# Macaron block: the last batch's row scatters and the second group's zero rows spread over the last run of blocks, the first group's zero rows moved behind a layer norm's factors

## The chip, the cores and the metric

One core of a Trainium2 chip. The metric is device time in microseconds, the median of the runs shown.

## The reference

Eight sequences of 256 tokens, 128 channels. Three sublayers, each on a layer norm (no learned scale) of the residual x:

```python
x = x + 0.5 * ffn(layernorm(x))
x = x + attention(layernorm(x))
x = x + 0.5 * ffn(layernorm(x))      # same weights as the first
```

The attention has 16 heads of 8 channels, rotary embedding, an ALiBi bias (0 for later keys, so it is not causal) and a projection with a bias. The feed-forward is a mixture of 8 experts, 128 to 352 and back, top 2 by a softmax over the router's 8 logits:

```python
scores = softmax(xt @ router_w); w, idx = top_k(scores, 2)
h = gelu(xt @ w1[e]) * (xt @ v1[e]);  y = h @ w2[e]
out = sum over the two chosen e of w * y + bias
```

## The kernel before, in words

The 2048 tokens are 16 tiles of 128 rows. Of the first feed-forward, four tiles are computed densely (all experts), which is the dense stage at the start. The other twelve, and all sixteen of the second feed-forward, are routed: each normalised row is written twice, with a number behind its 128 floats (516 bytes), into a buffer `xs[p]` in HBM, at a place (`pos`) that sorts rows by expert. The blocks of 128 rows of one expert are then loaded from there, sent through the expert, and the result rows are scattered to `yp[p]` by their numbers (`dest`). The last block of an expert is filled up with rows of zeros. There are three such phases p: 0 is the first feed-forward (31 blocks), 1 is batches 0 to 5 of the second (31 blocks), 2 is its batches 6 and 7 (15 blocks).

The order of the work is written out by hand, engine by engine. PE: dense stage; blocks 0 to 30; attention over batches b = 0 to 7, each in 16 slots s; then the last run of 46 blocks, 31 to 76, in steps i = 0 to 45 (`blocks(1)`). During batch b, the layer norm and routing of the batch before for the second feed-forward are fitted in. The rest of batch 7 (projection, layer norm, routing) lies inside the first steps of the last run (`last_attention`).

A block passes through: load by SP (L418, six slots, three blocks a group); three transposes on PE for a group (L1462); an exact split into high and low parts, ACT (L756) and DVE (L1131 next to it copies `dest`); up projections on PE (L1472 to L1474); gelu on ACT (L783), product on DVE (L1156); transposes of the hidden rows on PE (L1483), copies out on DVE (L1137) and ACT (L763); down projection on PE (L1490); copy of y on ACT (L770); scatter of y on POOL (L538).

`y_copy` of block n waits until the scatter of block n - 3 has landed (three slots `ysb`), and the transposes L1483 of a block wait for the copy of y of the block two before it (two banks). SP's first load of a phase waits in `rows_there` until all of the phase's row scatters and zero rows have landed and its table is made.

POOL issues all indirect DMAs, in its one order:

- `scatter(r, c, ...)` (L523, DMA at L531): one DMA for each copy k of each tile, so four for a batch of two tiles. `scatter2(b)` is called for it in the second feed-forward.
- `zero_scatter(p)` (L569): two DMAs, 128 single rows (L573) and 128 groups of 8 rows, 4,128 bytes each (L576), 528 KB in all.
- `y_scatter(n)` (L535, DMA at L538): 128 rows of 512 bytes.

In the pass of POOL's loop for batch 7 it issues: `scatter2(5)`, `zero_scatter(1)`, two iotas (`number_pairs(6)`), the layer norm's factors of batch 6 (`rstd_of`, four small operations L516 to L521), an iota, `copy_again(6)`. After the loop comes `scatter2(6)`, and then the last run: `y_scatter` of each block, with batch 7's four row scatters behind those of steps 8 and 9, two each, `zero_scatter(2)` behind that of step 10, and four additions to the residual (`add_ffn_bias`, L593) behind steps 12 to 15. What those feed: SP's load of block 62 (the first of phase 2, used by PE in step 30), and DVE's `combine`, which begins in step 38.

Of the kernel before, what the change touches and what calls it, by code (L numbers as in the profile page):

```python
# [14 lines left out]
B, N, D = 8, 256, 128  # L15
P = 128
TB = N // P
NT = B * TB
# [28 lines left out]
ZG = 8  # L47
# [74 lines left out]
def macaron(nc, x, small_w, w1, v1, w2, ffn_bias, proj_b, slopes, ident, dist, dist_t, rope, expert_ids,  # L122
            far, ones_rows, out):
    ctx = ExitStack()
    with ctx:
        ctx.enter_context(nc.allow_low_precision(reason="exact splits"))

        def sb(name, shape, dt=F32):
            return ctx.enter_context(nc.sbuf_tensor(name, shape, dt))

        def sem(name):
            return ctx.enter_context(nc.semaphore(name))

        def sems(name, n):
            return [ctx.enter_context(nc.semaphore(f"{name}{i}")) for i in range(n)]
# [104 lines left out]
        zpos = sb("zpos", [P, 2, 1], U32)  # L240
# [18 lines left out]
        xs = [nc.dram_tensor(f"xs{r}", (BLOCK_ROWS * P + P, XW), F32, kind="Internal").ap() for r in range(3)]  # L259
# [42 lines left out]
        zstep, zero_landed, zmem = sems("zstep", 2), sems("zero_landed", 2), sem("zmem")  # L302
# [3 lines left out]
        scat1, scat2 = sem("scat1"), sems("scat2", 2)  # L306
# [39 lines left out]
        def xn2_twice(b, k):  # L346

            return ((xn2_again_l if b >= SPLIT else xn2_again) if k else xn2)[:, b % 2]
# [162 lines left out]
        def _(pool):  # L511
            def rstd_of(w, c, first_tile, tiles):

                t = slice(first_tile, first_tile + tiles)
                pool.wait_ge(mean_done[w], (c + 1) * tiles)
                nc.gpsimd.tensor_scalar(rstd[:, t], mv[:, t, 1], EPS, None, ALU.add).then_inc(eps_done[w], 1)  # L516
                nc.gpsimd.tensor_scalar(nmr[:, t], mv[:, t, 0], -1.0, None, ALU.mult).then_inc(eps_done[w], 1)
                pool.wait_ge(eps_done[w], 2 * c + 2)
                nc.gpsimd.tensor_tensor(rstd[:, t], rstd[:, t], mhalf[:, 0:tiles], ALU.pow).then_inc(rstd_done[w], 1)
                pool.wait_ge(rstd_done[w], c + 1)  # L520
                nc.gpsimd.tensor_tensor(nmr[:, t], nmr[:, t], rstd[:, t], ALU.mult).then_inc(nmr_done[w], 1)  # L521

            def scatter(r, c, src, landed, tiles=None):  # L523

                T = CHUNKS[r][0]
                p = 2 if r and c >= SPLIT else r
                pool.wait_ge(pos_done[r], c + r)
                pool.wait_ge(again_done[r], c + r)
                for t in tiles or range(c * T, (c + 1) * T):
                    for k in range(2):  # L530
                        nc.gpsimd.indirect_dma_start(  # L531
                            out=xs[p][:, :], out_offset=bass.IndirectOffsetOnAxis(ap=pos[:, k, t:t + 1], axis=0),
                            in_=src(t, k), in_offset=None).then_inc(landed, 16)
# [8 lines left out]
            def number_pairs(b):  # L542

                if b >= 2:
                    pool.wait_ge(scat2[b % 2], 64 * (b // 2))
                for k in range(2):
                    nc.gpsimd.iota(xn2_twice(b, k)[:, :, D].bitcast(U32), [[P, TB]], base=b * 2 * N + k * N, channel_multiplier=1
                                   ).then_inc(numbers_at, 1)
# [6 lines left out]
            def split_qk(b, step):  # L555

                r, rs_ = (rc_e, rsn_e) if b < 2 else (rc, rsn)
                if step == 0:
                    pool.wait_ge(cos_done, b + 1)
                    pool.wait_ge(sin_done, b * 2 + 2)  # L560
                    nc.gpsimd.tensor_tensor(r, r, rs_, ALU.add).then_inc(split_step, 1)
                elif step == 1:
                    pool.wait_ge(split_step, b * 5 + 2)
                    nc.gpsimd.tensor_tensor(r, r, lev[:, 0], ALU.subtract).then_inc(split_step, 1)
                else:
                    pool.wait_ge(split_step, b * 5 + 4)
                    nc.gpsimd.tensor_tensor(lev[:, 2], r, lev[:, 1], ALU.subtract).then_inc(split_step, 1)

            def zero_scatter(p):  # L569
                r, zeros = min(p, 1), zero_rows2 if p else zero_rows1  # L570
                pool.wait_ge(zstep[r], 18 if p == 2 else 9)
                pool.wait_ge(numbered, 4 if p else 3)
                nc.gpsimd.indirect_dma_start(  # L573
                    out=xs[p][:, :], out_offset=bass.IndirectOffsetOnAxis(ap=zpos[:, 0, :], axis=0),
                    in_=zeros[:, ZG, :], in_offset=None).then_inc(zero_landed[r], 16)
                nc.gpsimd.indirect_dma_start(  # L576
                    out=xs[p].rearrange("(g z) d -> g (z d)", z=ZG),
                    out_offset=bass.IndirectOffsetOnAxis(ap=zpos[:, 1, :], axis=0),
                    in_=zeros[:, 0:ZG, :].rearrange("p z w -> p (z w)"), in_offset=None).then_inc(zero_landed[r], 16)

            def project_bias(b):

                pool.wait_ge(xn_done[1], 2 * b + 2)
                nc.gpsimd.tensor_tensor(xres[:, 2 * b:2 * b + 2, :], xres[:, 2 * b:2 * b + 2, :],
                                        pbias[:, None, :].broadcast_to([P, TB, D]), ALU.add).then_inc(pb_added, 1)

            def add_ffn_bias(r, q):
                if q == 0:
                    if r == 0:
                        nc.gpsimd.tensor_scalar(hbias[:, :], hbias[:, :], 0.5, None, ALU.mult).then_inc(half_done, 1)  # L590
                        pool.wait_ge(half_done, 1)
                pool.wait_ge(xn_done[2 * r], 4 * q + 4)
                nc.gpsimd.tensor_tensor(xres[:, 4 * q:4 * q + 4, :], xres[:, 4 * q:4 * q + 4, :],  # L593
                                        hbias[:, None, :].broadcast_to([P, 4, D]), ALU.add).then_inc(bias_added, 1)
# [43 lines left out]
            for c in range(1, 4):  # L638
                scatter(0, c, lambda t, k: xn1[:, t - DT, k, :], scat1)
            zero_scatter(0)  # L640
            for q in range(1, 4):
                add_ffn_bias(0, q)
# [31 lines left out]
                    split_qk(1, 2)  # L674

            rstd_of(1, 2, 4, TB)
            def scatter2(b, tiles=None):
                scatter(1, b, lambda t, k: xn2_twice(t // TB, k)[:, t % TB, :], scat2[b % 2], tiles)

            for b in range(B):  # L680
                if b + 2 < B:
                    project_bias(b + 2)
                if b >= 2:
                    scatter2(b - 2)
                if b == B - 1:
                    zero_scatter(1)
                if b == 0:
                    rstd_of(1, 3, 6, TB)
                if b + 2 < B:
                    for step in range(3):  # L690
                        split_qk(b + 2, step)
                if b >= 1:
                    number_pairs(b - 1)
                    rstd_of(2, b - 1, 2 * b - 2, TB)
                if b >= 1 and b + 3 < B:
                    rstd_of(1, b + 3, 2 * b + 6, TB)
                if b == B - 2:

                    pool.wait_ge(s2_full, 16 * (B - 2))
                    nc.gpsimd.memset(zero_rows2, 0.0).then_inc(zmem, 1)  # L700
                    pool.wait_ge(zmem, 7)
                    nc.gpsimd.iota(zero_rows2[:, :, D].bitcast(U32), [[1, ZG + 1]], base=SCRAP, channel_multiplier=ZR
                                   ).then_inc(numbered, 1)
                if b == B - 1:

                    pool.wait_ge(s2_full, 16 * (B - 1))
                    nc.gpsimd.iota(run[2][:, 0, :], [[REG, E]], base=0, channel_multiplier=0,
                                   allow_small_or_imprecise_dtypes=True).then_inc(numbered, 1)
                if b >= 1:
                    copy_again(b - 1)  # L710
            scatter2(B - 2)
            for n in range(FIRST[1], sum(NB)):
                y_scatter(n)
                i = n - FIRST[1]
                if i == 0:
                    number_pairs(B - 1)
                    rstd_of(2, B - 1, 2 * B - 2, TB)
                if i == 3:
                    copy_again(B - 1)
                if 8 <= i < 10:  # L720
                    scatter2(B - 1, [NT - 2 + i - 8])
                if i == 10:
                    zero_scatter(2)
                if 12 <= i < 16:
                    add_ffn_bias(1, i - 12)


        @block.scalar
# [1036 lines left out]
```

## Time and profile before

| | us |
|---|---|
| median of 3 runs | 482.81 |
| lowest, highest | 482.15, 485.86 |
| span of the profiled execution, first to last instruction | 502.7 |

No separate time of the profiled execution is given beside its span. The profile has for each engine its instructions in order of time, the idle time before each in brackets with what released it. "issue" there is idle time in which the engine waited for nothing that the profile shows, and "remote", like "another core or an unknown queue", a release whose source has no record. The granted clock of TensorE is 1.00 at 2.4 GHz and 0.50 at 1.2 GHz. Some records can be missing.

### The profile page before, as it was taken

The numbers are of one execution on the slowest core, as the hardware profiler recorded it, in microseconds if no ns is written. First come the engines' busy times: TensorE is split into PE (matmuls) and PEld (weight loads), VectorE is DVE, ScalarE is ACT, GpSimd is POOL, SyncE is SP. The second block draws the span as 40 slices with busy tenths as digits, with TensorE's granted clock in tenths as the row PEclk, the third lists the DMA queues.
The fourth block names the chain that finished last, engine by engine and source line by source line (L and its number), as shares of the span: only waits on it lengthen the run. The fifth ranks groups of instructions, "written<-read, shape, count | busy, mean of one in ns | idle before, by whom it ended". The sixth has DMA issues, their size and how long they took to land.

```text
span 502.7 us, 10906 instructions
## 1 busy us (share of the span) xinstructions
PE 441.0 (88%) x3447; PEld 369.0 (73%) x3447; DVE 311.2 (62%) x935; ACT 248.2 (49%) x585; POOL 237.4 (47%) x321
## 2 busy tenths in 40 slices
PE   1998859899999898699999999999779969999990
PEld 1877648788899775577777777777459958888880
DVE  3765645976867485295959586756526744544672
ACT  4744434436444456255556565555465524554541
POOL 7365658556453413044454545432525467534441
PEclk9999959999999999899999999999999989999997
DMA  8971111122331010230212120200112223122522
GB/s 236 290 116 38 48 58 33 50 75 75 91 85 54 30 48 15 71 85 17 60 50 61 47 63 30 64 24 3 70 37 61 64 60 96 53 65 72 171 80 78
DMA packets 50633, 35.51 MB, mean 71 GB/s; under 512 B 5754, under 2 KB 47706, under 8 KB 50538
## 3 DMA queue, kind: packets, MB, share of 16 engines
q1 hardware_dynamic: 45140, 23.90, 18.9%
q0 software_dynamic: 4784, 10.54, 6.3%
q8 instruction: 30, 0.49, 0.4%
q10 hardware_dynamic: 656, 0.40, 0.3%
q14 instruction: 23, 0.19, 0.1%
HBM read 15.37 MB, written 13.01 MB: 56 GB/s over the span
## 4 chain that ended last, share of the span: by engine, by line
PE 65%; DVE 9%; issue 8%; ACT 5%; POOL 4%; DMA 3%; another core or an unknown queue 2%; ACTq 1%; SPq 1%; POOLq 0%; DVEq 0%
PE bank L1490 9%; PE bank L1483 6%; PE bank L1587 5%; PE bank L1472 5%; PE bank L1473 4%; PE bank L1474 4%; PE bank L1626 4%; PE bank L1611 4%; PE bank L1444 3%; PE bank L1590 2%; PE bank L1591 2%; PE bank L1462 2%; PE bank L1614 2%; PE bank L1434 2%
## 5 line engine op out<-in xcount | busy, mean ns | idle before, releaser
L538 POOL DMA_INDIRECT yp<-scr,dest x77 | 76.5, 994 | 90.8 <-ACT scr L770 71.1
L877 ACT ACTIVATE stage<-bank 128x512 f32<-128x512 f32 x128 | 74.6, 597 | 72.6 <-PE bank L1615 63.7
L1263 DVE TENSOR_REDUCE nm<-bank 128x2 f32<-128x512 f32 x128 | 84.0, 685 | 38.4 <-PE bank L1591 35.8
L1490 PE MATMUL bank<-wd,scr 128*128 (+1 forms) x462 | 64.9, 277 | 1.3 <-ACT scr L763 1.3
L1472 PE MATMUL bank<-wu,xbT 128*128 x154 | 63.1, 410 | 2.1 <-DVE xbT L1129 1.8
L1137 DVE COPY scr<-bank 128x256 f32<-128x256 f32 x77 | 32.5, 422 | 51.5 <-PE bank L1483 22.8
L1490 PEld LDWEIGHTS bank<-wd,scr 128*128 128x128 f32 (+1 forms) x462 | 60.7, 193 | 1.8 <-issue 1.7
L1587 PE MATMUL bank<-qk_rows 126*128 126x256 bf16 x256 | 50.8, 280 | 4.9 <-DMA qk_rows<-lev 4.2
L1611 PE MATMUL bank<-qk_rows 128*128 128x256 bf16 x256 | 50.3, 279 | 3.7 <-DMA qk_rows<-wd 3.0
L1473 PE MATMUL bank<-wu,xbT 128*128 x154 | 50.8, 330 | 0.0
L1474 PE MATMUL bank<-wu,xbT 128*128 x154 | 50.8, 330 | 0.0
L783 ACT ACTIVATE scr<-bank 128x352 f32<-128x352 f32 x77 | 35.7, 463 | 29.1 <-PE bank L1474 21.7
L1483 PE MATMUL bank<-idn,scr 128*128 128x128 f32 (+1 forms) x231 | 40.1, 283 | 10.0 <-ACT scr L770 8.7
L1614 PE MATMUL bank<-near_hi,idn_r 128*128 128x256 f32 x128 | 47.3, 369 | 0.0
L1590 PE MATMUL bank<-near_hi,idn_r 128*128 128x256 f32 x128 | 47.0, 367 | 0.0
L1156 DVE TENSOR_TENSOR scr<-bank,scr 128x352 f32<-128x352 f32 x77 | 40.1, 521 | 9.4 <-ACT scr L783 2.1
L763 ACT ACTIVATE scr<-bank 96x128 f32<-96x128 f32 x77 | 21.0, 273 | 47.9 <-DVE scr L1137 33.9
L1483 PEld LDWEIGHTS bank<-idn,scr 128*128 128x128 f32 (+1 forms) x231 | 25.1, 138 | 23.0 <-issue 14.7
L1615 PE MATMUL bank<-near_lo,idn_r 128*128 128x256 f32 x128 | 36.0, 281 | 0.0
L1591 PE MATMUL bank<-near_lo,idn_r 128*128 128x256 f32 x128 | 35.8, 280 | 0.0
L531 POOL DMA_INDIRECT xs<-qk_rows,pos x28 | 27.4, 980 | 15.9 <-issue 9.9
L1626 PE MATMUL bank<-stage,vaug 128*9 128x256 f32 x512 | 34.2, 385 | 0.4 <-ACT stage L877 0.4
(218 smaller groups left out, 949.3 us busy)
## 6 DMA issues: line engine op xcount, KB each, us to landing
qk_rows<-lev SPq DMA_DIRECT2D x96, 64.0 KB
scr<-xs SPq DMA_DIRECT2D x77, 64.5 KB
stage<-yp SPq DMA_DIRECT2D x8, 256.0 KB, 3.2
scr<-yp SPq DMA_DIRECT2D x6, 256.0 KB, 3.1
stage<-in_w SPq DMA_DIRECT2D x8, 176.0 KB, 3.4
stage<-in_v SPq DMA_DIRECT2D x8, 176.0 KB, 4.3
xs<-qk_rows SPq DMA_DIRECT2D x3, 451.5 KB
yp<-scr,dest POOLq DMA_INDIRECT x77
```

The lines of the kernel that those rows point to most:

```text
L538: nc.gpsimd.indirect_dma_start(out=yp[PHASE[n]][:, :], out_offset=bass.IndirectOffsetOnAxis(ap=dest[:, n:n + 1], axis=0), in_=ysb[:, n % Y ...
L877: nc.scalar.activation(probs[:, g % RING, kt, 2 * (hp % 2):2 * (hp % 2) + 2, :], psS2[(b * 16 + j) % 3][:, :].rearrange("p (h n) -> p h n" ...
L1263: nc.vector.tensor_reduce(nm[:, qt, 2 * hp:2 * hp + 2], psS1[i % 2][:, :].rearrange("p (h n) -> p h n", h=2), AX.X, ALU.max, negate=True). ...
L1472: nc.tensor.matmul(dst, hi, moving(n, a), start=True, stop=False)
L1473: nc.tensor.matmul(dst, lo, moving(n, a), start=False, stop=False)
L1474: nc.tensor.matmul(dst, hi, moving(n, a + 2 * F), start=False, stop=True).then_inc(done, 1)
L1483: i = nc.tensor.transpose(ph[n % len(ph)][0:w, k * P:(k + 1) * P], hid[:, n % 2, f:f + w], idn[:, :])
L1490: i = nc.tensor.matmul(ph[n % len(ph)][:, 3 * P:4 * P], hTs[0:w, n % 2, k * P:(k + 1) * P], wd[0:w, bass.ds(experts[n], 1), k, :].rearrang ...
L1587: nc.tensor.matmul(o[:, j * N:(j + 1) * N], qs[b % RING][0:S1_ROWS, h, qt * P:(qt + 1) * P], ks[b % RING][0:S1_ROWS, h, :], start=(j == 0) ...
L1590: nc.tensor.matmul(o, idn_r[:, :], near_hi[0][:, 2 * hp:2 * hp + 2, :], start=False, stop=False)
L1611: nc.tensor.matmul(o[:, a * N:(a + 1) * N], ks[b % RING][0:S2_ROWS, h, kt * P:(kt + 1) * P], qs[b % RING][0:S2_ROWS, h, :], start=(a == 0) ...
L1614: nc.tensor.matmul(o, idn_r[:, :], near_hi[1][:, 2 * hp:2 * hp + 2, :], start=False, stop=False)
```

## The change

- Batch 7's four row scatters, before behind `y_scatter` of steps 8, 8, 9, 9, are issued one each behind steps 8, 10, 12 and 14. `scatter` and `scatter2` get a parameter `copies` for it.
- The two DMAs of `zero_scatter(2)`, before both behind step 10, are issued behind steps 17 and 20 (`half`).
- The four additions `add_ffn_bias(1, q)` move from steps 12 to 15 to steps 21 to 24.
- `zero_scatter(1)` moves from before `number_pairs(6)` and `rstd_of(2, 6, ...)` to behind them.

No DMA or instruction is added or removed.

```diff
-            def scatter(r, c, src, landed, tiles=None):
+            def scatter(r, c, src, landed, tiles=None, copies=range(2)):
...
-                    for k in range(2):
+                    for k in copies:
...
-            def zero_scatter(p):
+            def zero_scatter(p, half=None):
...
+                if half != 1:
+                    nc.gpsimd.indirect_dma_start(... zpos[:, 0, :] ...)
+                if half != 0:
+                    nc.gpsimd.indirect_dma_start(... zpos[:, 1, :] ...)
...
                 if b >= 2:
                     scatter2(b - 2)
-                if b == B - 1:
-                    zero_scatter(1)
                 if b == 0:
                     rstd_of(1, 3, 6, TB)
...
                 if b >= 1:
                     number_pairs(b - 1)
                     rstd_of(2, b - 1, 2 * b - 2, TB)
+                if b == B - 1:
+                    zero_scatter(1)
...
-                if 8 <= i < 10:
-                    scatter2(B - 1, [NT - 2 + i - 8])
-                if i == 10:
-                    zero_scatter(2)
-                if 12 <= i < 16:
-                    add_ffn_bias(1, i - 12)
+                if i in (8, 10, 12, 14):
+                    scatter2(B - 1, [NT - 2 + (i - 8) // 4], [(i - 8) // 2 % 2])
+                if i in (17, 20):
+                    zero_scatter(2, (i - 17) // 3)
+                if 21 <= i < 25:
+                    add_ffn_bias(1, i - 21)
```

## Rows read from the trace of the kernel before

**Rows 1.** The page: span, busy shares, and the chain that ended last.

```profile
span 502.7 us, 10906 instructions
...
PE 441.0 (88%) x3447; PEld 369.0 (73%) x3447; DVE 311.2 (62%) x935; ACT 248.2 (49%) x585; POOL 237.4 (47%) x321
...
PE 65%; DVE 9%; issue 8%; ACT 5%; POOL 4%; DMA 3%; another core or an unknown queue 2%; ACTq 1%; SPq 1%; POOLq 0%; DVEq 0%
```

**Rows 2.** Busy time by stretch: four bursts of DMAs on POOL.

```profile
core 0: us, PE busy (x) PEld busy (x) DVE busy (x) ACT busy (x) POOL busy (x), PEclk, DMA share, GB/s
...
54.87:67.20 12.33, 7.83 (x49) 6.33 (x47) 6.42 (x24) 3.59 (x10) 9.57 (x10) 0.92 0.15 49
234.50:239.40 4.90, 4.90 (x42) 4.39 (x39) 2.78 (x6) 2.23 (x5) 3.97 (x4) 1.00 0.12 40
354.31:362.40 8.09, 4.81 (x47) 3.48 (x46) 4.17 (x18) 4.17 (x9) 6.55 (x7) 0.99 0.14 44
402.20:411.30 9.10, 4.28 (x31) 3.76 (x31) 3.60 (x14) 2.20 (x7) 5.75 (x6) 0.93 0.24 68
```

**Rows 3.** POOL in order of time, in the last run of blocks.

```profile
402.22 0.96 POOL L538 DMA_INDIRECT yp<-scr,dest  x1 [1.56 <-ACT scr L770]
...
406.01 0.96 POOL L538 DMA_INDIRECT yp<-scr,dest  x1 [0.30 <-issue]
...
408.53 0.96 POOL L531 DMA_INDIRECT xs<-qk_rows,pos  x1 [0.30 <-issue]
411.36 0.96 POOL L538 DMA_INDIRECT yp<-scr,dest  x1 [1.86 <-ACT scr L770]
...
419.40 1.29 POOL L593 TENSOR_TENSOR xres<-xres,hbias 128x512 f32<-128x512 f32 x1
```

**Rows 4.** PE in order of time in the same stretch: the transposes of hid.

```profile
411.23 0.87 PE L1483 MATMUL bank<-idn,scr 128*128 128x128 f32 x3 [4.39 <-ACT scr L770]
...
415.58 0.84 PE L1483 MATMUL bank<-idn,scr 128*128 128x128 f32 x3
...
418.29 0.52 PE L1483 MATMUL bank<-idn,scr 128*128 128x128 f32 x3
...
420.43 0.52 PE L1483 MATMUL bank<-idn,scr 128*128 128x128 f32 x3
```

**Rows 5.** ACT there: the copy of y that PE waited for.

```profile
410.80 0.28 ACT L770 ACTIVATE scr<-bank 128x128 f32<-128x128 f32 x1 [2.15 <-remote]
```

**Rows 6.** Busy time of each engine in two stretches at half clock.

```profile
362.20:365.70 3.50, 3.28 (x24) 2.10 (x24) 1.12 (x5) 1.25 (x3) 0.99 (x6) 0.51 0.37 151
410.00:416.90 6.90, 5.67 (x24) 5.54 (x25) 2.44 (x8) 2.13 (x6) 3.83 (x4) 0.51 0.30 107
```

**Rows 7.** POOL in order of time, last attention batch.

```profile
361.38 0.96 POOL L576 DMA_INDIRECT xs<-qk_rows,zpos  x1 [0.30 <-issue]
...
366.35 0.20 POOL L521 TENSOR_TENSOR nmr<-nmr,rstd 128x2 f32<-128x2 f32 x1
```

**Rows 8.** PE in order of time, last attention batch to the last run.

```profile
362.42 1.22 PE L1650 MATMUL bank<-wsm,scr 128*128 128x128 f32 x4 [2.55 <-issue]
...
373.93 0.52 PE L1462 MATMUL bank<-idn,scr 128*128 128x128 f32 x3 [0.35 <-issue]
```

**Rows 9.** ACT in the dense stage: gelus 1, 23 and 24.

```profile
15.69 0.60 ACT L842 ACTIVATE scr<-bank 128x512 f32<-128x512 f32 x1
...
84.21 0.60 ACT L842 ACTIVATE scr<-bank 128x512 f32<-128x512 f32 x1 [1.10 <-PE bank L1436]
...
86.50 0.59 ACT L842 ACTIVATE scr<-bank 96x512 f32<-96x512 f32 x1 [1.11 <-PE bank L1436]
```

**Rows 10.** What DMA moved, in 40 slices of 0.3 us from 361 us on.

```profile
GB/s 0 0 220 0 0 0 303 385 399 427 248 0 0 0 0 0 0 0 41 157 59 141 78 136 50 46 172 29 131 96 181 5 0 0 0 0 0 0 0 0
```

**Rows 11.** SP issuing loads, up to 367 us: the first three.

```profile
365.59 1.53 SPq L418 DMA_DIRECT2D scr<-xs  x3
```

**Rows 12.** The chain that ended last: the last y scatter's data.

```profile
492.22 2.33 DMA yp<-scr,dest
```

More of the change, by code:

```diff
@@ L572, in zero_scatter @@
                 pool.wait_ge(numbered, 4 if p else 3)
[L573 to L579, printed above, removed]
+                if half != 1:
+                    nc.gpsimd.indirect_dma_start(
+                        out=xs[p][:, :], out_offset=bass.IndirectOffsetOnAxis(ap=zpos[:, 0, :], axis=0),
+                        in_=zeros[:, ZG, :], in_offset=None).then_inc(zero_landed[r], 16)
+                if half != 0:
+                    nc.gpsimd.indirect_dma_start(
+                        out=xs[p].rearrange("(g z) d -> g (z d)", z=ZG),
+                        out_offset=bass.IndirectOffsetOnAxis(ap=zpos[:, 1, :], axis=0),
+                        in_=zeros[:, 0:ZG, :].rearrange("p z w -> p (z w)"), in_offset=None).then_inc(zero_landed[r], 16)
             def project_bias(b):
@@ L676, in _, with scatter2 @@
             rstd_of(1, 2, 4, TB)
-            def scatter2(b, tiles=None):
-                scatter(1, b, lambda t, k: xn2_twice(t // TB, k)[:, t % TB, :], scat2[b % 2], tiles)
+            def scatter2(b, tiles=None, copies=range(2)):
+                scatter(1, b, lambda t, k: xn2_twice(t // TB, k)[:, t % TB, :], scat2[b % 2], tiles, copies)
             for b in range(B):
```

## Prediction

> **What bounds the kernel now.** I read the page first: PE is busy 88% of a span of 502.7 us and holds 65% of the chain that ended last, but "issue" and an unknown source together hold 10% of that chain [rows 1]. So the question is where PE stands still for reasons no engine explains. I then went through POOL in order of time, looked for its bursts of DMAs, and asked for the busy time of each engine in those stretches [rows 2]. The reader is to see this: in a burst of four DMAs (234.50 to 239.40, the ordinary batch; there are five like it before 340 us) PE is busy 4.90 us of 4.90. In the burst that four row scatters make with the first group's two zero DMAs, PE is busy 4.81 of 8.09; in the burst of the last run 4.28 of 9.10; in the dense stage's longest, of ten, 7.83 of 12.33. Short bursts cost nothing, long ones stop PE in their later half.
>
> The last run's burst in detail: POOL's six DMAs from 402.22 to 409.49 follow one another with 0.30 us between [rows 3]; PE stands for 4.39 us before the transposes at 411.23 [rows 4], released by ACT's copy of y at 410.80, which itself stood 2.15 us for a "remote" release [rows 5]. That copy has two waits, the down projection on PE and the landing of a scatter of y issued eleven microseconds earlier, both over by then; its source has no record. After it the clock is granted at 0.51 for the stretch 410.0 to 416.9 [rows 6]. The other: PE stands 2.55 us until 362.42, put down to "issue" [rows 8], and the clock is 0.51 from 362.2 to 365.7 [rows 6].
>
> **Are these stalls in the timed runs too?** The profiled execution took 502.7 us, the median of the runs is 482.81: 19.9 us of the span (or more, since what lies around the span is only in the timed run) are not there without the recorder. PE's steady stretches run at the full clock and nothing can be taken from them. The dense stage goes from gelu 1 at 15.69 to gelu 24 at 86.50, 70.8 us; at the undisturbed 2.29 us of its last step [rows 9] 23 steps take 52.7. So 18.1 us are over there, most of it around bursts. With the two stalls above (11.0 us, below) that makes 29.1 us of stalls, against 19.9 us that the timed runs don't have. If all of the excess is stalls, (29.1 - 19.9) / 29.1 = 0.32 of a traced stall is real; some of the dense stage's 18.1 us are ordinary waits for loads and routing, which lowers that. I take 0.25. The ends are 0 (the recorder alone makes them) and 1.
>
> A rule of the Trainium skill bears on this (NOTIFIC — the notification-queue block, section 7.1): the block that writes trace records holds back its sources rather than lose a record inside, and that can throttle an engine. The "remote" releases without a record [rows 5] fit it and don't prove it; by that rule alone the share is 0 and the sum below comes to 483.9. Another page speaks against it (Runtime: NRT & Kernel Launch, on the preamble and postamble): a profile's total is about 6.2 us above the reported time for reasons of its own. If this span contained that, only 13.7 us of the excess were stalls, the share were 0.53 and the sum near 478; no row here shows it.
>
> **Part 1, the last run.** Nothing is removed: six DMAs and four additions are moved.
> - The stall. PE lost 4.39 us [rows 4]. Behind it, two blocks at half clock: 411.23 to 415.58 is 4.35 us, where such a step, with the transposes of a group, takes some 0.4 more than 2.14, say 2.5, and 415.58 to 418.29 is 2.71 against 2.14 from 418.29 to 420.43 [rows 4]: 1.8 + 0.6 = 2.4. Together 6.8 us in the trace.
> - The new order. A block takes 2.14 us or, every third, 2.5; a DMA on POOL 0.96 + 0.30 = 1.26 [rows 3]. With one more behind every second block POOL is busy 3.8 of some 4.5 us and has at most three in a row, fewer than the four that cost nothing [rows 2]. So the stall goes whole.
> - A true wait that goes, recorder or not. Without the stall, the scatters would follow at 1.26 us: step 9's at 406.01, step 10's at 409.8, the zeros at 411.1 and 412.3, step 11's at 413.6. The zeros' data take 2.9 us (below), so step 11's rows, in the same queue behind them, land near 416.2. The copy of y in step 14's turn, six blocks after that of step 8 (402.0 at latest, since its scatter began at 402.22 [rows 3]), is due at 402.0 + 6 x 2.27 = 415.6. So about 0.6 us of real waiting, passed on to PE. Bounds: 0 (a scatter passes the zeros' data) and 1.8 (each addition of 1.29 us [rows 3] pushes the next scatter as well; those four fall 3 to 4.3 us behind their copies, against a slack of 6.8 - 0.3 - 2.3 = 4.2 us, the 2.33 being a scatter's data [rows 12]). Afterwards, the additions lie behind steps 21 to 24 and start from no backlog: at most some 2 us late, hidden by the same slack.
> - The zeros in steps 17 and 20 must have landed before SP loads block 62, which PE wants in step 30; at 2.9 us of data behind step 20 they have over seven steps, 15 us. Batch 7's rows land by step 16. Both hidden. The additions are wanted in step 38. Hidden too. If I am wrong on the queue, the cost is a load that waits, not PE.
>
> **Part 2, the first group's zeros.** They leave a burst of six, which becomes a burst of four like those that cost nothing [rows 2]. In the trace this gives 2.55 us [rows 8] and half of the 3.28 busy us at half clock [rows 6], 1.6: 4.2 together. Lower bound 0, if PE then waits for the same chain through ACT.
>
> What it costs. Before, the large zero DMA is issued at 361.38 [rows 7] and its data move until 364.3: the slices at 303 to 427 GB/s, the seventh to the eleventh of 0.3 us from 361 [rows 10]. SP waits for that. It issues three loads from 365.59 on [rows 11]; the 193.5 KB of the three have moved seven slices after the traffic begins at 366.4, at 368.5 [rows 10]. PE wants them at 373.93 [rows 8]: 5.4 us in hand. After, the pair starts when the factors are done, 366.35 + 0.20 = 366.55 [rows 7]: large DMA at 366.55 + 0.30 + 0.96 + 0.30 = 368.1, data gone at + 2.9 = 371.0, three loads there at + 4.2 = 375.2. PE's own work behind the factors doesn't shrink (366.55 to 373.93 is 7.4 us, nearly all at full clock), and if the stall before is gone both move forward together. So PE waits 375.2 - 373.9 = 1.3 us at the head of the last run, and nothing covers it: all 46 blocks stand behind that load. With a quarter chance that the idle brings one more stretch at half clock like [rows 6], 0.4. I take 1.7; bounds 0 (SP answers the last landing at once, which saves the 1.3 us from 364.3 to 365.59) and 3.3 (1.3 + 1.6 + 0.4 of semaphores). Also queued behind the two DMAs on POOL are an iota and `copy_again(6)`, half a microsecond later than now, before row scatters that begin at 375: hidden.
>
> **Sum.** In the trace: 502.7 - 6.8 - 4.2 + 1.7 = 493.4. For the median: a quarter of 11.0 is 2.75; 482.81 - 2.75 - 0.6 + 1.7 = 481.2 us.
>
> **Rivals.**
> 1. The stalls are real in timed runs (share 1). For it: engines stop in every long burst in the same way, and the clock falls, which is no artefact of records. Against it: the 19.9 us, and the missing source. 482.81 - 11.0 + 1.7 = 473.5.
> 2. The late zeros take over (slower). Place: SP's wait at the head of the last run. Stalls all the recorder's, the queue's wait 0, the full 3.3 us: 486.1. If the landing comes 1.7 us later still, because the zeros' data now meet the attention's last work, it passes the 1% bound: near 488. It decides from the point where zeros land more than 3.1 us after the factors (373.93 less 4.2 us of loads, less 366.55). For it: the 5.4 us in hand and the 6.7 us by which the DMA moves are both in rows. Against: the loads may be issued quicker.
> 3. The change does nothing that counts: the stalls are the recorder's, and the true wait and the late zeros cancel: 482.8.
>
> **How the numbers follow.** Forecast (share near a quarter, 479 to 484.5) 0.50; rival 1 and shares above one half 0.23; rival 2 0.14, half of it above the 1% bound; rival 3 0.13. A change under 1% is what a measurement of this kernel can hardly tell from none. Faster by over 1% (under 478.0): rival 1, 0.23, and a little of the forecast's lower end, 0.02: 0.25. Slower by over 1% (above 487.6): 0.07. Within: 0.68. The range leaves out the far ends of rivals 1 and 2: 474.5 to 486.
>
> **What would show it.** In the changed kernel's profile, POOL should have no run of more than four DMAs behind 350 us; PE's gaps of 4.39 and 2.55 us and their stretches at 0.51 should be gone; SP's first load of the last run should start near 372 by today's clock (5 to 6 us behind the factors) and the transposes L1462 behind it should wait over 1 us for a DMA. The forecast is wrong if the span shrinks by 9 us and the time as well (rival 1), if the time rises although the stalls went (rival 2), or if a new PE gap shows at steps 20 to 25.

## The result and the profile after

The changed kernel takes 488.04 us (median of 12 runs, 485.73 to 490.21) against 483.82 us for the kernel before (12 runs, 482.15 to 486.98). The ratio on record is 1.0077, 95% interval 1.0051 to 1.0103: 0.8% slower, some 3.7 us. (The two medians are 4.2 us apart; this text goes by the ratio.) The forecast was 481.2 us, no change or slightly faster, range 474.5 to 486.0; the time lies outside it, near what rival 2 gave (486.1 to 488). The kernel before itself measured 1.0 us above the 482.81 us of three runs that the sum began with.

The profiled execution of the changed kernel, the page's first line and its chain by engine (for [rows 1]):

```profile
span 486.1 us, 10909 instructions
...
PE 56%; DVE 7%; DMA 6%; issue 5%; ACT 5%; POOL 3%; SPq 2%; ACTq 1%; POOLq 0%; DVEq 0%
```

Its span is 486.1 us beside a timed 488.01 of the same execution: 1.9 us lie around the span. By that, as an estimate, the execution profiled before, 502.7 us [rows 1], would have had a time of 504.6, while none of the 12 timed runs is above 486.98. The "remote" share of the chain is gone. DMA has 6% of it where it had 3%, and the wait at the head of the last run is in it. The chain from the factors of the layer norm to the last run's first transposes (columns: start, us, what; "..." stands for lines left out):

```profile
353.99 0.20 POOL nmr L521
354.18 0.53 issue
354.71 1.08 POOL xs L574
355.79 0.30 issue
356.10 3.33 DMA xs<-qk_rows,zpos
...
359.56 0.47 SPq L351
...
360.30 0.35 SPq L418
...
361.50 1.85 DMA scr<-xs
363.35 0.27 issue
363.62 0.89 PE bank L1464 x3
```

PE has nothing else to do while this chain runs out, from 360.22 on: factors done at 354.19, small zero DMA, large zero DMA, 3.33 us until its data have landed, SP reads the table and issues three loads, the third takes 1.85 us to land, PE transposes. In the kernel before the large zero DMA was issued ahead of the factors, and all of this lay under the attention's last slots.

PE in order of time, the same transposes (for [rows 8], where they waited 0.35 us):

```profile
363.62 0.87 PE L1464 MATMUL bank<-idn,scr 128*128 128x128 f32 x3 [3.40 <-DMA scr<-xs]
...
369.28 0.49 PE L1485 MATMUL bank<-idn,scr 128*128 128x128 f32 x3
```

And the busy time by stretch behind the wait (for [rows 6]; PE first, PEclk the third figure from the end):

```profile
363.60:369.10 5.50, 4.22 (x15) 3.78 (x16) 1.46 (x5) 2.24 (x3) 2.32 (x3) 0.50 0.49 111
369.10:380.00 10.90, 10.90 (x83) 10.22 (x83) 7.64 (x24) 6.38 (x19) 4.61 (x9) 1.00 0.16 41
```

The granted clock is 0.50 from 362.3, while PE still waits, until 369.1, so the first blocks run at half clock. In the last run POOL now has at most three DMAs in a row (for [rows 3]), and PE's transposes there follow at 2.13 and 2.5 us without a gap (the next wait is 0.57 us for a load, at 455.36):

```profile
405.77 0.95 POOL L538 DMA_INDIRECT yp<-scr,dest  x1 [1.17 <-ACT scr L772]
407.03 0.96 POOL L531 DMA_INDIRECT xs<-qk_rows,pos  x1 [0.30 <-issue]
408.29 0.95 POOL L538 DMA_INDIRECT yp<-scr,dest  x1 [0.30 <-issue]
410.03 0.96 POOL L538 DMA_INDIRECT yp<-scr,dest  x1 [0.79 <-ACT scr L772]
```

### The profile page after: what moved, and what is told of

Same layout as the page of the kernel before. It is cut to its first block, busy times and chain, and to the rows that moved or that the text cites. A ratio compares the mean times of both kernels' runs of the same rounds, so it can differ in the third digit from the quotient of the medians.

```text
span 486.1 us, 10909 instructions
## 1 busy us (share of the span) xinstructions
PE 435.6 (90%) x3447; PEld 365.4 (75%) x3447; DVE 313.7 (65%) x935; ACT 248.1 (51%) x585; POOL 236.7 (49%) x321
## 4 chain that ended last, share of the span: by engine, by line
PE 56%; DVE 7%; DMA 6%; issue 5%; ACT 5%; POOL 3%; SPq 2%; ACTq 1%; POOLq 0%; DVEq 0%
PE bank L1492 8%; PE bank L1485 6%; PE bank L1589 5%; PE bank L1474 4%; PE bank L1475 4%; PE bank L1476 4%; PE bank L1613 4%; PE bank L1628 4%; PE bank L1592 3%; PE bank L1593 2%; PE bank L1464 2%; PE bank L1616 2%; PE bank L1617 2%; DMA scr<-xs 2%; DMA qk_rows<-wd 2%
## 5 line engine op out<-in xcount | busy, mean ns | idle before, releaser
L1628 PE MATMUL bank<-stage,vaug 128*9 128x256 f32 x512 | 35.2, 395 | 0.4 <-ACT stage L879 0.4
L772 ACT ACTIVATE scr<-bank 128x128 f32<-128x128 f32 x77 | 21.3, 276 | 23.9 <-PE bank L1492 23.9
```

## The experiments

Two theories at the start. Late zeros: the loss is the first group's zero rows, whose landing nothing covers any more. Spreading: the DMAs put between the blocks cost. Ratios are to the kernel before, timed beside each version on the same chip, with the 95% interval. Where two versions are compared with each other by their ratios, both intervals count.

### The kernel before, profiled again

No edit.

> The kernel before itself, for a second profile and for what no change measures as. If the two long stalls (PE 4.39 us at 406 to 411, 2.55 us at 360 to 362) and the dense stage's 18 us belong to one profiled execution alone, this profile's span lies near 482 us and PE has no gap over 1 us in either place. If they come with every profile, the span is again near 500 and the gaps are there. Ratio to the kernel before 1.000, within 0.002.

Measured: 483.94 us against 484.02, ratio 1.0007 (0.9981 to 1.0034). The second profile, first line of the page, and PE and ACT in the last run:

```profile
span 479.9 us, 10906 instructions
```

```profile
396.55 0.52 PE L1483 MATMUL bank<-idn,scr 128*128 128x128 f32 x3
399.92 0.52 PE L1483 MATMUL bank<-idn,scr 128*128 128x128 f32 x3 [0.83 <-ACT scr L770]
402.06 0.52 PE L1483 MATMUL bank<-idn,scr 128*128 128x128 f32 x3
```

```profile
399.50 0.28 ACT L770 ACTIVATE scr<-bank 128x128 f32<-128x128 f32 x1 [1.03 <-DMA yp<-scr,dest]
```

The same kernel, 22.8 us shorter in its span: the stalls of 4.39 and 2.55 us [rows 4, 8] are not in this execution, and POOL here issues eleven DMAs with 0.30 us between, 385.57 to 399.17, in the same place. So long bursts do not stop PE. What the burst does here is the small true wait of the prediction: step 14's copy of y waits 1.03 us for a scatter to land (step 11's, issued at 396.95), and PE 0.83 us for the copy.

The dense stage, too, was stretched in the first profile alone. Gelus 1 and 24 in the second (for [rows 9], where they stand at 15.69 and 86.50):

```profile
15.68 0.60 ACT L842 ACTIVATE scr<-bank 128x512 f32<-128x512 f32 x1
...
73.91 0.59 ACT L842 ACTIVATE scr<-bank 96x512 f32<-96x512 f32 x1 [1.11 <-PE bank L1436]
```

It takes 58.2 us and not 70.8: 12.6 us of the 22.8 lie here. In all profiles but the first it is 57.6 to 58.9 us, the changed kernel's too. So of the 18.1 us above the ideal 52.7, some 5.5 are in every profile.

### One part at a time

Only the last run's part (`e1`), which takes back in the changed kernel:

```diff
                     scatter2(b - 2)
+                if b == B - 1:
+                    zero_scatter(1)
...
                     rstd_of(2, b - 1, 2 * b - 2, TB)
-                if b == B - 1:
-                    zero_scatter(1)
```

> Only the last run's part of the change: the first group's zeros back ahead of the layer norm's factors. Theory (late zeros): the whole loss lies in them, so this is as fast as the kernel before or up to 0.6 us faster, ratio 0.998 to 1.001, and PE has no wait for a load at the head of the last run. Rival (spreading): the DMAs between the blocks cost, ratio 1.005 or more.

Only the first group's zeros (`e2`), the opposite edit on the kernel before:

> Only the first group's zeros moved, the last run as before. Late zeros: ratio 1.008 (3.7 us: a wait of 3 us or more for the first load, and one more stretch at half clock). Spreading: ratio 1.000 to 1.002.

Measured: e1 483.32 us, ratio 0.9982 (0.9960 to 1.0004); e2 488.08 us, ratio 1.0087 (1.0069 to 1.0106). The last run's first transposes in e1, then in e2:

```profile
359.91 0.52 PE L1464 MATMUL bank<-idn,scr 128*128 128x128 f32 x3 [0.35 <-issue]
```

```profile
361.80 0.52 PE L1462 MATMUL bank<-idn,scr 128*128 128x128 f32 x3 [3.45 <-DMA scr<-xs]
```

In e2 PE waits 3.45 us for the first loads, and the clock is 0.50 for 6.8 us there; in e1 the transposes wait 0.35 us as before. The loss is the second part's, whole. Spreading costs nothing: its ratio is what PE's 0.83 us would give, though the interval just reaches 1.

### The landing moved earlier and later

`e4`, the changed kernel with the large DMA of the pair ahead of the factors and the small one behind:

```diff
+                if b == B - 1:
+                    zero_scatter(1, 1)
...
-                    zero_scatter(1)
+                    zero_scatter(1, 0)
```

> The changed kernel with the large zero DMA back ahead of the factors and only the small one (128 rows) behind them. Late zeros: the small one starts at the changed kernel's 354.7 and lands about 2.3 us later instead of at 359.4, so SP loads 2.4 us earlier; the wait for the first load falls from 3.4 to about 1 us and the loss to a third, ratio 1.002 to 1.004. If only the order against the factors counts and not the landing, the ratio stays at 1.008.

`e5`, the kernel before with the pair one step later than the change has it:

```diff
                 if b >= 1:
                     copy_again(b - 1)
+                if b == B - 1:
+                    zero_scatter(1)
```

> The kernel before with the first group's zeros one step later than the change puts them: behind copy_again(6), which waits for the normalised rows. Late zeros with nothing to cover them: PE's wait for the first load grows by what the large zero DMA starts later (about 0.9 us by the changed kernel's rows), so 4.3 us against 3.4, and the time by as much, ratio 1.010 to 1.011. If the loss came from the clock alone or from the factors' place, it stays at 1.0087.

Measured: e4 484.37 us, ratio 0.9995 (0.9965 to 1.0026), e5 490.04 us, ratio 1.0104 (1.0067 to 1.0142). The first transposes of the last run in e4 and in e5:

```profile
359.88 0.52 PE L1466 MATMUL bank<-idn,scr 128*128 128x128 f32 x3 [1.23 <-DMA scr<-xs]
```

```profile
364.19 0.88 PE L1462 MATMUL bank<-idn,scr 128*128 128x128 f32 x3 [4.72 <-DMA scr<-xs]
```

The landing of the pair's last DMA sets the wait, not the factors' place. The last DMA starts 1.91 us behind the end of the factors in the changed kernel and 3.21 us behind it in e5 (353.43 to 356.64): 1.30 us more, and the wait grows by 1.32. Nothing absorbs any of it. (In time e5 is 1.0104 beside e2's 1.0087; that difference is inside the noise.) In e4 the last DMA starts 0.52 us behind the factors (352.62 to 353.14), and being the small one it is also done sooner: 6.74 us from its start to PE's transposes and not 7.52. Of the 2.17 us less wait, 1.39 are the earlier start and 0.78 the smaller DMA. e4's time is better than I expected (1.002 to 1.004, of which its interval holds the lower part): its wait, 0.88 us above the 0.35 of e1, is about what the spreading gives back.

### The clock behind the wait

PE is kept at work where it waits by matmuls whose result nothing reads, into a bank that is free there. `e6` is the changed kernel with 28 of them before the first transposes and 10 behind; `e7` is e1 with 2 and 10; `e10` the kernel before with 2 and 10.

```diff
+            def keep_busy(n):
+                for _ in range(n):
+                    nc.tensor.matmul(bank[0][:, 0:N], ks[1][0:S2_ROWS, 0, 0:P], qs[1][0:S2_ROWS, 0, :], start=True, stop=True)
...
             ranks(1, B - 2, rank2)
+            keep_busy(28)
             blocks(1)
...
                 xbT(GROUP_OF[first])
+                if r == 1:
+                    keep_busy(10)
```

> The changed kernel with PE kept at work while it waits at the head of the last run: 28 matmuls of 256 columns into a bank that is free then, before the first transposes, and 10 behind them (in the 1.26 us in which it waits for DVE); none of them is used. They make the wait no shorter. If the fall to half clock (0.50 from 362.3 to 369.1) is a part of the loss, the clock stays at 1.00 there and the time falls by 1.5 to 2.5 us against the changed kernel, ratio to before 1.003 to 1.005. If the clock costs nothing, the ratio stays at 1.008.

> Only the last run's part of the change (as in e1), with PE kept at work at the head of the last run by 2 unused matmuls before the first transposes and 10 behind them. The clock was 0.50 for 3.4 us there in e1's profile and 1.00 in the second profile of the kernel before; if it falls in most executions, this is worth some 1.4 us (the first transposes of a hidden row 4.1 us behind PE's arrival and not 5.5) on top of e1's 0.9: ratio 0.995 to 0.997. If it falls seldom, ratio 0.998 as e1.

> The kernel before with nothing but the 2 and 10 unused matmuls at the head of the last run. e7 was at 0.9951 with both parts, e1 at 0.9982 with the spreading alone. If the two add, this is at 0.997 (1.4 us, when the fall to half clock behind 361 us comes in nearly all executions); if it comes in few, 0.999 or more.

Measured: e6 485.71 us, ratio 1.0020 (0.9993 to 1.0046). PE, and the busy time behind the wait, in e6's profile:

```profile
363.59 0.52 PE L1468 MATMUL bank<-idn,scr 128*128 128x128 f32 x3 [0.99 <-DMA scr<-xs]
...
367.36 0.49 PE L1489 MATMUL bank<-idn,scr 128*128 128x128 f32 x3
```

```profile
363.60:369.10 5.50, 5.33 (x40) 4.81 (x41) 2.63 (x8) 3.36 (x6) 1.92 (x2) 1.00 0.41 97
```

The loads come no sooner: counted from the end of the factors (353.48), the transposes start 10.11 us later and not 9.43, because the third load took 2.56 us in this execution and not 1.85. The 0.99 us are what the 28 matmuls left of the wait. The clock stays at 1.00, and the first transposes of hidden rows come 3.77 us behind those of the input and not 5.66 (363.62 to 369.28 above). So 1.89 us of the loss are the half clock. The time agrees, less sharply: the medians are 2.3 us apart, the ratios 0.0057, which is 2.8 us with an interval of some 1.0 to 4.6 (estimate from the two intervals). Over the timed runs the mean granted clock is 0.985 in e6 and 0.976 in the changed kernel (medians of 12), so the fall is not a matter of the profiled execution alone.

e7: 482.30 us, ratio 0.9951 (0.9923 to 0.9979). e10: 484.33 us, ratio 0.9998 (0.9969 to 1.0027), though in its profile too the clock stays at 1.00 behind 357 us. What the half clock at the head costs the kernel before is seen in the profiles only. Of five profiles in which the first load is on time and no matmuls are added, three have 0.50 for 3.4 us there (the first profile of the kernel before, e1, e8) and two have none (its second profile, e9). In the three the first transposes of hidden rows come 1.1 to 1.5 us later. None of the five profiles with the added matmuls (e6, e7, e10, and e11 and e12 below) has it. The mean of the five, 0.8 us, is less than e10's interval can tell from nothing.

### Which move in the last run gives the gain

`e8` has only the rows spread, `e9` only the zeros and the additions later (both from the kernel before). As in e1, the first group's zeros stay ahead of the factors.

> The kernel before with batch 7's row scatters alone spread over steps 8, 10, 12 and 14; the second group's zeros behind step 10 and the additions behind steps 12 to 15 stay. The kernel before lost 0.83 us to one wait in its second profile (transposes 3.37 us apart instead of 2.55). If it is POOL's backlog of six DMAs that makes the copy of y wait, the gap goes here; if it is the zeros' data in front of a scatter in the queue, with the additions behind, it stays, 0.5 to 1 us. In time both are within noise: ratio 0.997 to 1.002.

> The kernel before with the second group's zeros behind steps 17 and 20 and the additions behind steps 21 to 24, but batch 7's four row scatters still behind steps 8 and 9, two each. e8 has lost PE's 0.83 us gap with the rows alone spread, so a backlog is behind it and not the zeros' data alone. Here POOL's run is six DMAs (three of blocks, four rows, less the two zeros) and the gap shrinks below 0.4 us or goes, if the backlog needs both. If the row scatters alone make it, it stays at 0.8. Time within noise either way, ratio 0.997 to 1.001.

Measured: e8 484.66 us, 0.9997 (0.9962 to 1.0032); e9 482.83 us, 0.9974 (0.9951 to 0.9996). What e9's expectation says of e8, that the gap had gone, was a misreading: it had only shrunk and moved. PE in e8, then in e9:

```profile
408.39 0.52 PE L1485 MATMUL bank<-idn,scr 128*128 128x128 f32 x3
411.23 0.52 PE L1485 MATMUL bank<-idn,scr 128*128 128x128 f32 x3 [0.69 <-ACT scr L772]
413.60 0.52 PE L1485 MATMUL bank<-idn,scr 128*128 128x128 f32 x3 [0.21 <-ACT scr L772]
```

```profile
391.58 0.52 PE L1485 MATMUL bank<-idn,scr 128*128 128x128 f32 x3
393.71 0.52 PE L1485 MATMUL bank<-idn,scr 128*128 128x128 f32 x3
395.84 0.52 PE L1485 MATMUL bank<-idn,scr 128*128 128x128 f32 x3
398.39 0.52 PE L1485 MATMUL bank<-idn,scr 128*128 128x128 f32 x3
```

e8 still has 0.69 + 0.21 us, e9 none, although POOL issues ten DMAs in one go there (384.90 to 397.22). The other profiles bear it out: the wait of 0.8 to 0.9 us is in all four that have the last run as before (e0, e2, e5, e10), and in none of the eight in which the zeros and additions come later. The zeros and additions behind the rows make the backlog that reaches the copy of y; the bunched rows alone don't. Moving rows apart was not needed. Zeros and additions were not told apart by a run; in e0 the first addition (399.18) begins only after step 11's scatter, so there the two zero DMAs' places in POOL's order did it. In time e8 and e9 are not clear of each other.

### A version that beats both

e7 once more, and e9 with the same unused matmuls:

> e7 a second time (last run's part alone, PE kept at work at its head), since e10 says that the unused matmuls alone are worth nothing in time and e1 gave the spreading 0.9982: if the two add, this is at 0.998, and e7's 0.9951 was luck of the draw; if it is real, 0.994 to 0.997 again.

> e9 (only the second group's zeros and the additions moved to later steps, rows bunched as before) with PE kept at work at the head of the last run. e9 had no gap of PE left and 0.9974. If the unused matmuls help, 0.995 or 0.996; if not, 0.997 to 0.998 as e9.

Measured: 482.19 us, 0.9934 (0.9911 to 0.9958), and 482.86 us, 0.9943 (0.9917 to 0.9969). e7, e11 and e12 are faster than the kernel before by 0.5 to 0.7%, each with an interval clear of 1, and over 1% faster than the changed kernel. The single gains, of e1 or e9 (0.2 to 0.3%) and of the matmuls (nothing in e10), add up to 0.2 or 0.3%, which is less. But each of the three intervals that meet in such a comparison is 0.2 to 0.3% to either side, so the gap is hardly larger than the noise, and whether the two parts help each other is not shown. What can be seen is the clock: its median over the timed runs is 0.0025 to 0.003 above the kernel before's in e7, e11 and e12, and not above it in e10 (0.9825 beside 0.984).

## Why the prediction was wrong

**The share of the stalls (2.75 us of gain) was wrong at its root.** "I take 0.25" gave a quarter of 11.0 us. The runs show 0: the second profile of the kernel before has neither stall, nor has any other profile of a version, and its slowest timed run beside any of them took 489.86 us, not 504. The stalls belonged to one profiled execution. What caused them there stays open: the second profile has the same burst without them, and since no later execution showed them, the recorder's part could not be tested. The reading "short bursts cost nothing, long ones stop PE" [rows 2] was a pattern inside that one execution. Eleven DMAs in a row in e0 and ten in e9 refute it. The argument from 502.7 against 482.81 pointed the right way and should have been carried to the end. What kept it from there is the dense stage: the text took all of the 18.1 us above the ideal as candidates, of which 5.5 are in every profile. With the 12.6 that are not, the stalls are 12.6 + 11.0 = 23.6 us, against 22.8 us between the two spans: next to nothing is left for a real share. The 13.7 us that the text tried as a smaller excess fall away too: an execution's time is 1.9 us above its span, not below it.

**The wait at the head of the last run (1.3 us) was the step that decided, and it was mis-sized: 3.3 us.** The mechanism, its place and its chain were as written. Two terms were off. The first is the work that PE has left behind the factors, "366.55 to 373.93 is 7.4 us". In the second profile of the kernel before it is 352.80 to 358.91, 6.1 us:

```profile
352.60 0.20 POOL L521 TENSOR_TENSOR nmr<-nmr,rstd 128x2 f32<-128x2 f32 x1
```

```profile
358.91 0.52 PE L1462 MATMUL bank<-idn,scr 128*128 128x128 f32 x3 [0.35 <-issue]
...
362.68 0.49 PE L1483 MATMUL bank<-idn,scr 128*128 128x128 f32 x3
```

The 7.4 us themselves ran at full clock, as the text says:

```profile
366.55:373.93 7.38, 5.96 (x67) 4.02 (x66) 1.99 (x15) 5.29 (x11) 0.49 (x2) 1.00 0.22 54
```

But the stretch just ahead of them did not. From the projection's matmuls L1650 that feed the factors (362.42 [rows 8]; 348.86 in the second profile) the factors end 4.1 and 3.9 us later, while PE reaches the last run's transposes 11.5 and 10.1 us later: after its stall PE worked at 0.51 until 365.7 [rows 6] and was behind its place when the factors were done. So 1.3 us of the slack was the disturbed execution's. The second term is the chain behind the factors: 8.65 us by my sum, and 363.62 - 354.19 = 9.43 as measured. The first DMA starts 0.53 us behind the factors and not 0.30 and takes 1.08 us and not 0.96, and it is 3.33 us from the start of the large one to its landing where I had counted 2.9 of data. That is 0.8 us. 1.3 + 1.3 + 0.8 = 3.4, against 9.43 - 6.11 = 3.3.

**The half clock (0.4 us) was given a quarter chance and came**, in all three profiles with a wait of over 3 us (the changed kernel, e2, e5). It was also priced too low: 1.6 us in the text, 1.89 us by e6. The kernel before pays 0 to 1.5 us of the same kind.

**The true wait for a slot of y (0.6 us) was right**: 0.83 us in e0, in the copy of step 14 and for step 11's rows, as worked out. One step of its working did not hold: step 11's rows did not queue behind the zeros' data. Their own data took 2.47 us (396.95 to 399.42), about the usual 2.33 [rows 12]; they were late because POOL issued them late. That the sum came out close owes something to luck. The hidden moves of part 1 were hidden: no gap in steps 20 to 25.

Together: the transposes come 3.3 us later behind the factors, + 1.89 of clock, - 0.83 of the wait that went = 4.4 us; less what the kernel before pays for half clock itself, 0.8 on the mean of five profiles, = 3.6. Measured: 3.7 by the ratio, 4.2 by the medians. Of the 6.8 us between forecast and time, 1.0 is the kernel before's own time, 2.75 the stalls, 2.0 the wait and 0.7 the half clock (1.89 less the 0.4 forecast and the 0.8 that the kernel before pays), less 0.2 by which the wait that went was larger than forecast. That makes 6.2 or 6.3; the rest is what lies between the ratio and the medians.

**Rival 2** had the place and the mechanism, and its point of decision (zeros landed more than 3.1 us behind the factors) holds: they landed 5.2 us behind. But the forecast's own numbers (data gone at 371.0, 4.45 us behind) were past that point too, so it did not tell the two apart. Rival 2 got 0.14 where it deserved most, since its price was made with the same slack from a disturbed stretch.

## What to carry to other kernels

Before a stall of a trace enters a sum, hold the profiled span against the timed runs. If the span is longer by as much as the stalls, take none of them, and take a second profile before measuring any slack near them: engines that a stall has put out of step with each other show a slack that isn't there. When a DMA is moved behind something, write its whole chain down to the engine that consumes it (issue, landing, the loader's reaction, the load) and compare it with the work that the waiting engine has left. What sticks out was paid one to one here, and the half clock came on top. When a burst of small DMAs makes an engine late, try first to move the ones that nobody waits for soon. Here it was the zeros and additions that mattered, not the rows.

## What was not expected of the hardware

One profiled execution can differ from the rest of the same program by 22.8 us in its span (502.7 and 479.9), with PE standing and ACT and DVE nearly so (PE 0, ACT 0.27 and DVE 0.94 us busy from 408 to 410), and with releases without a record. And unused matmuls in a wait can be worth their place: 38 of them kept the granted clock at 1.00 where it had been 0.50 for 6.8 us, which was worth 1.89 us in the trace and 2.3 us between the medians.
